# Token attention stage: where the quotients, the output's transpose and the output's moments stand in each engine's order

## The reference

```
x = x + _layernorm(_L0_attn_ref(_layernorm(x)))

raw    = einsum('bhid,bhjd->bhij', q, k)              # 16 heads of 8
scores = alpha * tanh(raw / beta) + lam * hamming + lat   # hamming, lat: bilinear in tanh(x @ bits)
scores = where(causal, scores, -inf)
attn   = softmax(scores)
out    = einsum('bhij,bhjd->bhid', attn, v) @ out_w.T
```

## Time and profile before

| | |
|---|---|
| median of 3 runs | 4018.34 us (4014.23 to 4018.38) |
| profiled execution, own time | 4016.93 us |
| its span | 4015.0 us, of which token attention is about the first 810 us |
| busy over the span | PE 3818.9, DVE 2970.6, ACT 2679.1, POOL 1953.6 us |
| one steady step of token attention | 23.97 us |

### The profile page before, as it was taken

The page is one execution under the profiler, slowest core; times in us unless marked ns, Lnnn a source line. Parts: engine busy times, 40 slices in busy tenths (PEclk is TensorE's granted clock), DMA queues, the critical chain, the costliest instruction groups (busy, mean ns, idle before and its releaser), DMA issues. The chain is left out here.

```text
span 4015.0 us, 104324 instructions
## 1 busy us (share of the span) xinstructions
PE 3818.9 (95%) x34969; PEld 2916.1 (73%) x34969; DVE 2970.6 (74%) x7017; ACT 2679.1 (67%) x6409; POOL 1953.6 (49%) x1930
## 2 busy tenths in 40 slices
PE   7999999879999989999999989999999999999999
PEld 5777777647777755677777557777777777789998
DVE  6899998869999955899997756555565556556666
ACT  7999999858788743788887346666666666633333
POOL 4666666667777721666665333333333334311111
PEclk9999999989999999999999999999999999999999
DMA  3000000000000011000000110000000000000000
GB/s 106 1 0 0 0 0 0 1 18 20 24 20 20 23 24 24 14 13 16 13 16 16 29 30 1 0 0 0 0 0 0 0 0 0 0 6 9 9 9 9
DMA packets 69051, 47.64 MB, mean 12 GB/s; under 512 B 38360, under 2 KB 57952, under 8 KB 68832
## 3 DMA queue, kind: packets, MB, share of 16 engines
q1 hardware_dynamic: 68960, 46.43, 4.5%
HBM read 12.62 MB, written 4.19 MB: 4 GB/s over the span
## 5 line engine op out<-in xcount | busy, mean ns | idle before, releaser
L1684 ACT ACTIVATE l_probs<-l_act,l_neg_max 128x128 f32<-128x128 f32 (+1 forms) x1024 | 416.2, 426 | 273.7 <-DVE l_neg_max L1641 271.1
L1621 POOL TENSOR_TENSOR l_probs<-l_probs,l_sums 128x512 f32<-128x512 f32 x384 | 391.6, 1041 | 365.7 <-DVE l_sums L1649 365.7
L409 POOL TENSOR_TENSOR t_probs<-t_probs,t_neg_max 128x512 f32<-128x512 f32 x384 | 391.6, 1042 | 251.1 <-DVE t_neg_max L478 251.0
L1641 DVE TENSOR_REDUCE l_neg_max<-l_act 128x2 f32<-128x512 f32 (+1 forms) x384 | 247.0, 685 | 356.1 <-PE l_act L1740 356.1
L2002 ACT ACTIVATE e_hT<-e_act 128x512 f32<-128x512 f32 x256 | 152.9, 597 | 285.2 <-PE e_act L2023 285.2
L468 DVE SCALAR_TENSOR_TENSOR t_probs<-t_tanh_qk,scalars_sb,t_dve 128x512 f32<-128x512 f32 x384 | 269.9, 744 | 66.9 <-ACT t_tanh_qk L573 35.9
L866 POOL TENSOR_TENSOR w_swappedQ<-w_rawQ,w_table 128x512 f32<-128x512 f32 x128 | 162.2, 1289 | 261.1 <-ACT w_rawQ L1083 261.1
L2035 PEld LDWEIGHTS e_dve<-e_sb,e_hT 128*128 128x128 f32 x2048 | 268.7, 191 | 13.4 <-ACT e_hT L2002 0.2
L866 POOL TENSOR_TENSOR w_swappedK<-w_rawK,w_table 128x512 f32<-128x512 f32 x128 | 228.7, 1808 | 92.7 <-ACT w_rawK L1083 92.7
L2035 PE MATMUL e_dve<-e_sb,e_hT 128*128 128x128 f32 x2048 | 269.9, 275 | 0.0
L2023 PE MATMUL e_act<-e_xnT,e_sb 128*128 128x256 f32 x1024 | 267.2, 384 | 0.0
(11 more groups left out here) (262 smaller groups left out, 10462.3 us busy)
## 6 DMA issues: line engine op xcount, KB each, us to landing
w_v_mid<-w_v SPq DMA_DIRECT2D x128, 130.0 KB, 2.3
z<-w_z_copy SPq DMA_DIRECT2D x32, 128.0 KB, 2.0
h<-z SPq DMA_DIRECT2D x32, 128.0 KB
out<-x_sb SPq DMA_DIRECT2D x32, 128.0 KB, 1.8
h<-z SPq DMA_DIRECT2D x32, 127.0 KB
wqkv_sb<-L_ffn_wqkv SPq DMA_DIRECT2D x2, 768.0 KB, 6.8
kv_up_sb<-L_attn_w_kv_up SPq DMA_DIRECT2D x1, 1024.0 KB, 9.5
e_sb<-L_ffn_w SPq DMA_DIRECT2D x1, 1024.0 KB, 5.5
```

The source lines that it names most:

```text
L409: nc.gpsimd.tensor_tensor(p, p, neg_max[:, j, 0:len(gs)].unsqueeze(2) .broadcast_to((P, len(gs), P * (t + 1))), ALU.add).then_inc(shifted. ...
L1621: nc.gpsimd.tensor_tensor(p, p, sums[:, at, 0:len(hs)].unsqueeze(2) .broadcast_to((P, len(hs), P * (t + 1))), ALU.mult).then_inc(divided.s ...
L1641: nc.vector.tensor_reduce(neg_max[:, units.index(name), 0:len(hs)], to_act.bank("s" + name, back)[:, :].rearrange("p (h j) -> p h j", h=le ...
L1684: ins = nc.scalar.activation(probs[:, at % SLOTS, s * width:(s + 1) * width], bank[:, s * width:(s + 1) * width], ACT.Exp, bias=neg_max[:, ...
```

## The change

Three places are moved; no instruction is added or taken away.

- In turn 3, DVE does `divide` of both tiles in front of `maxima` instead of behind it.
- In turn 4, TensorE transposes `o` directly behind the scores, in front of the transposes of the probabilities, and ACT copies `oT` in front of `pT`. The list `act_order` is changed alike.
- In turn 5, DVE takes the output's moments at the end of the turn, behind `maxima`, instead of at its start in front of `summed`; POOL's `norm.rsqrt` for them goes behind both subtractions of the turn, directly in front of `residual`. In turn 1 the input's moments keep their place; the lines around them only move.

```diff
--- before.py
+++ after.py
@@ -276,8 +276,8 @@
         act_order += ["raw" + name for name in units[2 * i:2 * i + 2]]
         dve_order += ["bil" + name for name in units[2 * i:2 * i + 2]]
         act_order += [jobs[i] for jobs in (VALUES, LATE_VALUES) if i in jobs]
+        act_order += ["oT"] if i == BACK else []
         act_order.append("pT" + units[2 * (i - LAG)])
-        act_order += ["oT"] if i == BACK else []
         dve_order.append("pT" + units[2 * (i - LAG) + 1])
         act_order += ahead_at.get(i, []) + front_at.get(i, []) + ([amid[i]] if i in amid else [])
         act_order += ["out"] if i == BACK else []
@@ -398,8 +398,6 @@
                             pool.wait_ge(centred.sem, centred.done("minus", ahead))
                             nc.gpsimd.tensor_tensor(center[:, :], center[:, :], norm.rstd[""][:, :], ALU.mult)\
                                 .then_inc(centred.sem, 1)
-                        if done and i == OUT:
-                            norm.rsqrt(pool, "y", done)
                         for name in twins(i) if back else []:
 
                             n, gs, t = unit(name)
@@ -411,6 +409,7 @@
                                 .broadcast_to((P, len(gs), P * (t + 1))), ALU.add).then_inc(shifted.sem, 1)
 
                         if done and i == OUT:
+                            norm.rsqrt(pool, "y", done)
                             residual(done)
 
                 pipeline(pool, n_seq, step, 4)
@@ -495,10 +494,6 @@
 
                 def step(ahead, front, back, done):
                     for i in range(turns):
-                        if done and i == OUT:
-
-                            wait_apart(nc, dve, c, to_act.drained.sem, to_act.drained.done("out", done))
-                            norm.post_copied_moments(dve, done, y)
                         if back:
                             summed(i, back)
                         j, seq = lagging(i, LAG, turns, back, done)
@@ -507,15 +502,19 @@
                             to_dve.wait_filled(dve, job, seq)
                             nc.vector.tensor_copy(pT[:, 2 * j + 1, :], to_dve.bank(job, seq)[:, :])\
                                 .then_inc(to_dve.drained.sem, 1)
+                        for t in range(TILES if done and i == DIVIDE else 0):
+                            divide(t, done)
                         if back:
                             maxima(i, back)
+                        if done and i == OUT:
+
+                            wait_apart(nc, dve, c, to_act.drained.sem, to_act.drained.done("out", done))
+                            norm.post_copied_moments(dve, done, y)
                         if ahead and i == MOMENTS:
                             if not ahead.first:
 
                                 dve.wait_ge(scaled.sem, scaled.done("xn1", ahead.before()))
                             norm.pre_moments(dve, ahead, x)
-                        for t in range(TILES if done and i == DIVIDE else 0):
-                            divide(t, done)
 
                 pipeline(dve, n_seq, step, 4, entered=lambda: c["x_rest"].wait(dve))
 
@@ -579,11 +578,11 @@
                                 half = int(jobs[i][2])
                                 taken(jobs[i], seq, yT[:, 2 * half:2 * half + 2, :]
                                       .rearrange("p a t -> p (a t)"), BANK)
+                        if done and i == BACK:
+                            taken("oT", done, oT[:, :], T)
                         j, seq = lagging(i, LAG, turns, back, done)
                         if seq:
                             taken("pT" + twins(j)[0], seq, pT[:, 2 * j, :], BANK)
-                        if done and i == BACK:
-                            taken("oT", done, oT[:, :], T)
                         j, seq = lagging(i, EXP, turns, back, done)
                         for name in twins(j) if seq else []:
                             act.wait_ge(shifted.sem, shifted.done(name, seq))
@@ -723,9 +722,6 @@
                         for jobs, seq in ((VALUES, back), (LATE_VALUES, done)):
                             if i in jobs and seq:
                                 values(jobs[i], seq)
-                        j, seq = lagging(i, LAG, turns, back, done)
-                        for name in twins(j) if seq else []:
-                            transposes(name, seq)
                         if done and i == BACK:
                             to_act.wait_free(pe, "oT", done)
                             to_dve.wait_drained(pe, "o1", done)
@@ -733,6 +729,9 @@
                                 ins = nc.tensor.transpose(to_act.bank("oT", done)[:, t * P:(t + 1) * P],
                                                           o[:, t], c["ident"][:, :])
                             ins.then_inc(to_act.filled.sem, 1)
+                        j, seq = lagging(i, LAG, turns, back, done)
+                        for name in twins(j) if seq else []:
+                            transposes(name, seq)
                         for jobs, seq in ((ahead_at, ahead), (front_at, front)):
                             for job in jobs.get(i, []) if seq else []:
                                 project(job, seq)
```

## The result

| | before | changed |
|---|---|---|
| median | 4017.07 us (6 runs, 4014.23 to 4022.82) | 4033.22 us (6 runs, 4024.40 to 4033.96) |
| ratio | | 1.0038, 95% interval 1.0027 to 1.0048 |
| profiled execution, span | 4015.0 us | 4022.5 us |
| steady step of token attention | 23.97 us | 24.48 us |

The change makes the kernel 16 us slower. In the table further down the medians are of all executions of a kernel, and ratio and interval leave out the slow ones, of which (1) and (5) had one each (5648.82 us at a granted clock of 0.63, 4088.27 us at 0.94); without them their medians are 4000.41 and 4018.51. The steady step here and in the table further down is the distance of ACT's first tanh between two steps that lie 20 steps apart, divided by 20.

A forecast was written before the change was run, and what follows sets the result against it. A loop through ACT, TensorE and DVE bounds the kernel, with POOL at 0.05 slack: -0.47 + 1.06 - 0.05 = 0.54 a step, taken as 0.55; 30 x 0.55 - 0.47 = 16.0 us, median 4034, range 4023 to 4042.

The forecast's parts named there:

- The loop and the slack: A loop through several engines sets the step; POOL's slack at the second exp of the next turn 1 is 0.05 us.
- The gain, 0.47: Turn 4: `oT` copied in the place of `pT` lets the output matmul start 0.47 us a step earlier.
- GpSimd's piece, +1.06: Step's end: var, rstd and the wait between turn 5's pair of subtractions and the residual add 1.06 us on POOL.
- The later maxima, 0 to 0.1 in ACT's slack: Maxima of turn 3 come 1.10 later; exp loses 0 to 0.1 us, absorbed by ACT's 0.69 of waiting, taken as 0.
- rival 3: Gain missing, loss whole: exp of turn 4 waits for maxima or `oT` is late; +1.0 a step, 4048; chance 0.08.
- The gain winning: Rival 1: POOL's piece stays hidden, step falls by 0.47, median 4004; needs added piece below 0.52 us; chance 0.08.
- Rival 2: Piece costs its spans, part of ACT's wait is given back later: -0.2 to +0.25 a step, 4012 to 4026; chance 0.07.
- The moments, "nothing on DVE", "with 0.10 over": End of turn 5 on DVE: the 0.87 us of moments fit the gap before the next turn 0's sum, 0.10 over.
- Exp's wait: Second exp of the next step's turn 1 on ACT waits about 1.0 us a step for POOL's subtraction.
- TensorE's idle time: Wait ahead of the output matmul goes near 0; TensorE instead waits for the sums in turns 2 and 3.
- The whole: Token stage: 30 boundaries of steps at +0.55 less one gain of 0.47 make 16.0 us; median 4034.

The follow-up runs named there:

- (1): Kernel before with only the quotients ahead of the maxima and `oT` first; moments and rsqrt as before: 4000.99 us, ratio 0.9955 to the kernel before.
- (5): Kernel before with only the transpose of `o` and copy `oT` first, quotients still behind the maxima: 4019.15 us, ratio 1.0006 to the kernel before.
- (3): Kernel before with only GpSimd's rsqrt moved behind the subtractions, DVE's moments at their old place: 4043.39 us, ratio 1.0065 to the kernel before.
- (4): Kernel before with only the quotients moved in front of the maxima: 4016.76 us, ratio 1.0002 to the kernel before.
- (7): Changed kernel with the residual deferred behind the next step's first pair of subtractions: 4004.84 us, ratio 0.9977 to the kernel before.
- (9): Changed kernel with the residual behind the next step's first pair and DVE's moments back at the sixth turn's start: 4000.63 us, ratio 0.9959 to the kernel before.
- (6): Changed kernel with two more small GpSimd operations behind the residual: 4048.23 us, ratio 1.0087 to the kernel before.
- (10): Changed kernel with DVE's moments back at the sixth turn's start, rsqrt still behind the subtractions: 4032.12 us, ratio 1.0037 to the kernel before.

## Why the prediction was right

Its forecast was 4034 us and slower with 0.85; measured 4033.22. Point by point:

- **The loop and the slack.** The step was cut at three places of the loop. From tanh of turn 2 to GpSimd's pair of turn 5 it was 221.19 - 205.49 = 15.70 and is 221.06 - 205.87 = 15.19: -0.51. From there to the next turn 0's pair 4.20, now 5.25: +1.05. From there to the next tanh of turn 2 it was 229.46 - 225.39 = 4.07, now 230.35 - 226.31 = 4.04: -0.03, the slack. The sum is +0.51 and the step grew by 0.51. Of the first -0.51, 0.03 lie ahead of the scores of turn 4 (6.17 behind tanh, now 6.14) and 0.48 between those and the output matmul.
- **The gain, 0.47.** Measured 0.48 at the output matmul and 0.485 alone in (1). The reason given, `oT` copied in the place of `pT`, held: the output matmul starts 0.43 behind the start of that copy, 0.45 before.
- **GpSimd's piece, +1.06.** Measured 1.05. The distance of starts in the last step was the right price; by the two spans (0.91) it would have been 0.39 to 0.40 a step. The Trainium skill (Perfetto Trace Analysis, GPSIMD Engine Instruction) advises to time GpSimd by the distance between starts and not by the spans, and the trace agrees: (3) costs 0.99 alone, and 0.91 - 0.05 would be 0.86. In the last step the 0.15 between the two prices are the gaps behind var and behind rstd, 0.07 and 0.08 us, each ahead of an instruction that waits for the one before it.
- **The later maxima, 0 to 0.1 in ACT's slack.** Measured 0 in (4), and rival 3 with it did not come.
- **Rivals.** The gain winning needed less than 0.52 us added to the piece. (7) and (9) are on that side: with the residual out of the piece the gain does win, at 4004.8 and 4000.6. Rival 2 had the wait given back later; (6) shows that nothing is given back.
- **The moments, "nothing on DVE", "with 0.10 over".** This step was wrong. The sum of turn 0 was due 0.95 behind tanh, as before (222.59 against 221.64), and came 1.29 behind it (222.79 against 221.50), 0.34 late, in every second step. The moments themselves fit as worked out: they end at 222.37 and the sum was due at 222.45. The working counted the instructions and not what lies between the last of them and the sum. That it did no harm to the forecast is luck: GpSimd was later still, as (10) shows; in (7) it costs 0.09 a step.
- **Exp's wait.** About 1.0 us a step was forecast; it stands idle 0.43 + 0.36 = 0.79 for GpSimd, and the second exp starts 2.08 behind the pair where 2.07 was taken.
- **TensorE's idle time.** It was to wait for the sums in turns 2 and 3. It waits 0.37 for the sum in turn 3 (at 207.59), but in turn 2 it waits 0.52 for `k`, which had not been foreseen and is late by the same wait of exp.
- **The whole.** 30 boundaries of 0.55 less one gain made 16.0. By the measured step it is 30 x 0.51 - 0.5 = 14.8; the token stage of the profiled execution is 13.8 longer and the medians differ by 16.2, with an interval of 4 us to both sides. The 0.04 a step was mis-sized mainly in the gain, 0.51 instead of 0.47 up to the pair. That 4034 met 4033.22 to a microsecond is closer than its terms are.

## What to carry to other kernels

An engine that is idle a third of the time can still hold the step, if its work stands in a dense piece whose end something waits for in order. Before moving an operation on such an engine, add up the piece from the last input that starts it to the first output that is waited for, and compare it with the slack there; here 0.05 us of slack stood against 1.06 us of moved work. And a change of several edits should be measured edit by edit: this one held 0.4% of gain under 0.7% of loss.

## What the runs showed that was not expected

In the kernels with the moments at the end of the sixth turn, DVE stands idle 0.42 to 0.43 us between the moments and the next step's first sum in every second step (0.49 the first time), and 0.04 to 0.06 in the others. The loop's body holds two steps, and the longer gap lies where the body ends and the next pass begins. Behind the last pass, where the program goes on instead of back, there is no gap. In (7):

```profile
737.63 0.24 DVE L189 BATCH_NORM_AGGREGATE t_ymv<-t_ystats 128x2 f32<-128x6 f32 x2
737.85 1.41 DVE L470 SCALAR_TENSOR_TENSOR t_probs<-t_tanh_qk,scalars_sb,t_dve 128x512 f32<-128x512 f32 x2
```

In the kernels with the maxima at that place the first sum is 0.95 behind tanh at the body's end and 0.92 inside it, 0.03 apart.

GpSimd shows the same in (6). There two 128x2 operations of 0.20 us, the second waiting for the first, stand last in the body. From the residual to the next pair it is 2.83 us at the body's end, 2.63 inside it and 2.65 behind the last pass. In the changed kernel the residual's last operation (0.73 us, waiting for the one before it) stands at that place, and it is 2.20 at both.

It looks as if the way back to the start of the body is hidden behind a long last instruction and not behind a short one (0.16 us on DVE, 0.20 on GpSimd) that itself waited for a semaphore. Two engines and the loop's exit bear this out, but what the engine does in that time was not shown, and a run with only the last instruction's length changed was not made. That the place costs 0.09 us a step is shown by (7) against (9).
